# Edge batches whose rows are fetched one by one on two queues: eleven batches instead of three, and an own side in fp32

## The reference

```python
theta = x[dst] - x[src]
w = sigmoid(relu(theta @ W1 + b1) @ W2 + b2)
agg = segment_sum(w * theta, dst)
indeg = segment_sum(ones, dst)
out = layernorm(x + agg + indeg * (x @ W4 + b4))
```

## Time and profile before

| | us |
|---|---|
| median of 3 executions | 3931.05 (3930.73 to 3932.52) |
| the profiled execution, its own time | 3929.44 |
| its span, first to last instruction | 3927.6 |
| busy: PE / PE weight load / DVE / ACT / POOL | 2018.4 / 1781.0 / 2979.7 / 1255.4 / 2953.8 |
| mean granted TensorE clock, share of full speed | 0.619 |

### The profile page before, as it was taken

How to read it: one execution, slowest core, us unless ns; L and a number is a source line. 1 busy time by engine, 2 the same in 40 slices (tenths; PEclk the granted TensorE clock), 3 DMA queues, 4 the chain that set the end, 5 groups by cost and what they waited for, 6 DMA issues and landing times.

```text
span 3927.6 us, 48444 instructions
## 1 busy us (share of the span) xinstructions
PE 2018.4 (51%) x10531; PEld 1781.0 (45%) x10531; DVE 2979.7 (76%) x4855; ACT 1255.4 (32%) x2220; POOL 2953.8 (75%) x3123
## 2 busy tenths in 40 slices
PE   3245555555545555555555555555555555555554
PEld 2244444444444444444444444444444444444444
DVE  7568777777777777777777777778778777777777
ACT  1223333333333333333333333333333333333332
POOL 7777777777777777777777777777777777777776
PEclk5565665566666556665666656666666665665666
DMA  7445455555555555555555545555555555555553
GB/s 234 131 138 148 144 147 143 146 147 147 147 147 147 147 147 148 146 148 147 147 147 143 148 145 147 147 146 148 148 146 147 147 148 145 146 148 144 149 147 105
DMA packets 343028, 577.99 MB, mean 147 GB/s; under 512 B 127642, under 2 KB 216768, under 8 KB 342501
## 3 DMA queue, kind: packets, MB, share of 16 engines
q0 software_dynamic: 147264, 399.12, 36.0%
q10 hardware_dynamic: 49501, 110.40, 8.7%
q1 hardware_dynamic: 145970, 65.36, 6.2%
HBM read 549.00 MB, written 31.99 MB: 148 GB/s over the span
## 4 chain that ended last, share of the span: by engine, by line
POOL 60%; issue 24%; DVE 8%; ACTq 4%; ACT 2%; DMA 1%; PE 0%; POOLq 0%; DVEq 0%
POOL arena L783 56%; POOL held_x L768 4%; ACTq L895 3%; DVE logit L1012 2%; DVE diff L1004 2%; DVE ps_both L998 1%; DMA arena<-table,lists 1%; ACT away L875 1%; ACTq L891 1%; DVE edge_rows L1027 1%; DVE edge_rows L1017 1%; ACT hot_ne L883 0%; ACT ps_log L902 0%; DVE square L976 0%; DVE rstd L978 0%
## 5 line engine op out<-in xcount | busy, mean ns | idle before, releaser
L783 POOL DMA_INDIRECT arena<-table,lists x2970 | 2810.2, 946 | 905.0 <-issue 899.5
L875 ACT ACTIVATE away<-dst_rows,neg_ids 126x896 bf16<-126x896 bf16 (+1 forms) x449 | 466.4, 1039 | 1587.6 <-issue 1587.6
L812 PE MATMUL ps_win<-edge_rows 128*128 128x130 f32 x3140 | 716.3, 416 | 424.7 <-DVE edge_rows L1027 406.7
L812 PE MATMUL ps_sum<-edge_rows 128*128 128x130 f32 x3136 | 713.4, 415 | 422.2 <-DVE edge_rows L1027 404.3
L812 PEld LDWEIGHTS ps_win<-edge_rows 128*128 128x128 f32 x3140 | 663.2, 319 | 482.8 <-issue 482.6
L812 PEld LDWEIGHTS ps_sum<-edge_rows 128*128 128x128 f32 x3136 | 660.1, 318 | 480.2 <-issue 479.6
L998 DVE TENSOR_TENSOR ps_both<-ps_both,arena 128x896 f32<-128x896 f32 x425 | 467.0, 1099 | 485.6 <-DMA arena<-table,lists 482.0
L794 PE MATMUL ps_both<-parts,hot_ne 126*128 126x128 bf16 x3138 | 334.3, 266 | 958.7 <-ACT hot_ne L883 633.7
L794 PEld LDWEIGHTS ps_both<-parts,hot_ne 126*128 126x128 bf16 x3138 | 245.9, 118 | 1072.1 <-issue 569.7
L1027 DVE TENSOR_TENSOR edge_rows<-arena,ps_log 128x896 f32<-128x896 f32 x425 | 461.5, 1086 | 129.2 <-ACT ps_log L902 129.0
L1004 DVE SCALAR_TENSOR_TENSOR diff<-ps_both,w_rows 128x896 f32<-128x896 f32 (+1 forms) x449 | 489.4, 1090 | 15.4
(11 more groups left out here) (136 smaller groups left out, 1198.6 us busy)
## 6 DMA issues: line engine op xcount, KB each, us to landing
dst_rows<-rel_of ACTq DMA_DIRECT2D x224, 441.0 KB
arena<-table,lists POOLq DMA_INDIRECT x2970
held_x<-table ACTq DMA_DIRECT2D x2688, 1.0 KB
parts<-parts_of SPq DMA_DIRECT2D x449, 31.5 KB
parts_of<-stage SPq DMA_DIRECT2D x112, 96.0 KB, 3.4
winT<-in_x_cols SPq DMA_DIRECT2D x112, 64.0 KB
window<-in_x SPq DMA_DIRECT2D x112, 64.0 KB
out<-yout SPq DMA_DIRECT2D x112, 64.0 KB
```

The source lines that it names most:

```text
L783: nc.gpsimd.indirect_dma_start(gath[:, slot_of(g) + t, :], None, table, ids)\
L812: last = nc.tensor.matmul(ps_sums(c), hot_en[:, b, t, :], scaled_x[:, b, t, :], start=(j == 0 and t == 0), stop=(stop and t == tiles_of(g) ...
L875: nc.scalar.activation(away[0:WK, b, 0:n], dst_rows[0:WK, p % 2, lo:lo + n], ACT.Abs, bias=neg_ids[0:WK, near_no(g):near_no(g) + 1]).then_ ...
```

## The change

The own side goes from three bf16 parts to one fp32 product over all 128 rows of the window. With it go `high`, `mid`, `take_high`, `low`, the store and the loads of parts, and the near lists. `hot_ne` becomes fp32 and `own` gets two buffers.

The batches fetched by hand become eleven. The number lists of all eleven go through DRAM (`hand_of`) into one partition (`hand_at`, two buffers). Of a batch's 896 rows SyncE fetches 500 and ScalarE 396: ScalarE 11 a batch from batch 42 on, during 396 batches, issued in three groups of 3, 4 and 4 around `distance` and `one_hot`; SyncE 56 a chunk from chunk 11 on, in runs of at most 28. `project_window(c + 2)` moves from j = 2 to j = 3, and `take_window(c + 2)` from j = 3 to j = 0 of the next chunk. SyncE's order for chunk c is now: load of window c + 1, a run of 28, result c - 1, the rest.

```diff
-HAND = 3
-HAND_FROM = 40
+HAND = 11
+HAND_FROM = 42
+SPAN = 36
+ACT_EACH = 11
+SP_ROWS = BATCH - ACT_EACH * SPAN
+SP_FROM = -(-HAND_FROM // NB)
+SP_LOAD = 28
+SP_EACH = 2 * SP_LOAD
...
+        def sync_rows(c):
+            lo = (c - SP_FROM) * SP_EACH
+            runs = []
+            for m, row in [divmod(n, SP_ROWS) for n in range(lo, lo + SP_EACH) if 0 <= n < HAND * SP_ROWS]:
+                if runs and runs[-1][0] == m and runs[-1][2] < SP_LOAD:
+                    runs[-1][2] += 1
+                else:
+                    runs.append([m, row, 1])
+            return runs
...
+        def hand_numbers(kind, m, row, n):
+            return nc.values_load_multi_w_load_instructions(
+                hand_at[0:1, m % 2, row:row + n], engines=[kind], min_val=0, max_val=z.nodes - 1,
...
+        def hand_transfer(eng, m, row, number):
+            p, t = divmod(row, BT)
+            eng.dma_start(hand_x[p:p + 1, m % 2, t, :], table[bass.ds(number, 1), :])\
+                .then_inc(hand_in[2 * m + row % 2], 16)
...
+        def fetch_by_sync(sp, m, row, n):
+            if row == 0:
+                sp.wait_ge(scaled, hand_free(m))
+                sp.wait_ge(hand_at_in[m % 2], 16 * (m // 2 + 1))
+                sp.sem_inc(sp_gate, 1)
+            for k, number in enumerate(hand_numbers(mybir.EngineType.SP, m, row, n)):
+                hand_transfer(sp, m, row + k, number)
...
-            for c in range(last_chunk + 1):
-                if c < last_chunk:
-                    store_parts(sp, c + 1)
-                if c:
-                    store_result(sp, c - 1)
-            store_result(sp, last_chunk)
+            store_numbers(sp)
+            for c in range(1, last_chunk):
+                wait(sp, rows_done, c - 1)
+                sp.wait_ge(win_ready, c)
+                sp.sem_inc(sp_gate, 1)
+                bases = clamped(base_i, c - 1, c + 2, z.last_base)
+                load_window(sp, c + 1, bases[2])
...
+                rows = sync_rows(c)
+                for m, row, n in rows[:1]:
+                    fetch_by_sync(sp, m, row, n)
+                store_result(sp, c - 1, bases[0])
+                for m, row, n in rows[1:]:
+                    fetch_by_sync(sp, m, row, n)
...
-                pe.wait_ge(parts_in[buf], 16 * (g // (2 * NB) + 1))
+                pe.wait_ge(own_ready, c + 1)
...
-                    last = nc.tensor.matmul(ps_z[b][:, t, :], hot_ne[0:WK, b, t * P:(t + 1) * P],
-                                            parts[0:WK, buf, :], start=True, stop=True)
+                    last = nc.tensor.matmul(ps_z[b][:, t, :], hot_ne[:, b, t * P:(t + 1) * P], own[:, c % 2, :],
+                                            start=True, stop=True)
...
-                if j == 2 and c + 2 <= last_chunk:
+                if j == 3 and c + 2 <= last_chunk:
                     project_window(c + 2)
                 add_up(g)
...
-                if hand_row(g):
-                    fetch_hand(*hand_row(g))
+                by_hand = hand_row(g)
+                if by_hand:
+                    numbers = load_hand(*by_hand)
+                    fetch_hand(*by_hand, numbers, 0)
                 if g + 3 < all_batches:
                     distance(g + 3)
+                if by_hand:
+                    fetch_hand(*by_hand, numbers, 1)
+                if g + 3 < all_batches:
                     one_hot(g + 3)
+                if by_hand:
+                    fetch_hand(*by_hand, numbers, 2)
...
-                if j == 3 and c + 2 <= last_chunk:
-                    take_window(c + 2)
+                if j == 0 and 0 < c < last_chunk:
+                    take_window(c + 1)
```

More of the change, by code:

```diff
@@ L14 @@
 EPS = 1e-5
-ROUND = 12582912.0
 BT = 7
@@ L34 @@
 SB = 3
-SLOTS = 4
 DB = 2
@@ L100, in __init__ @@
         self.held = [c * NB for c in self.held_chunks]
-        self.hand = [HAND_FROM + (P + 2) * (m + 1) + m for m in range(HAND)]
-        assert self.hand[-1] < self.batches and HAND_FROM > self.held[1] and not set(self.hand) & set(self.held)
+        self.hand = [HAND_FROM + SPAN * (m + 1) + 2 * NB - 1 for m in range(HAND)]
+        assert self.hand[-1] < self.batches and not set(self.hand) & set(self.held)
+        assert HAND_FROM > self.held[1] and HAND_FROM + SPAN > self.held[3] and SP_EACH * SPAN >= SP_ROWS * NB and\
+            SP_FROM + -(-HAND * SP_ROWS // SP_EACH) < self.chunks
         assert min(b - a for a, b in zip([0] + self.held, self.held)) >= PAIRS * STEPS and self.groups > 16
@@ L448, in hand_row, with hand_free @@
         def hand_row(g):
[L449 to L453, removed]
+            m, n = divmod(g - HAND_FROM, SPAN)
+            return (m, SP_ROWS + n * ACT_EACH) if 0 <= m < HAND else None
+        def sync_rows(c):
[7 more added lines that the diff above has]
+            return runs
+        def hand_free(m):
+            return (z.hand[m - 2] if m >= 2 else z.held[2 * m + 1]) + 1
+        def hand_numbers(kind, m, row, n):
+            return nc.values_load_multi_w_load_instructions(
+                hand_at[0:1, m % 2, row:row + n], engines=[kind], min_val=0, max_val=z.nodes - 1,
+                skip_runtime_bounds_check_because="src holds numbers of nodes")[1]
+        def hand_transfer(eng, m, row, number):
+            p, t = divmod(row, BT)
+            eng.dma_start(hand_x[p:p + 1, m % 2, t, :], table[bass.ds(number, 1), :])\
+                .then_inc(hand_in[2 * m + row % 2], 16)
         def held_step(g):
@@ L662, in clamped, with load_window, store_result @@
                 skip_runtime_bounds_check_because="place_bases clamps it to this range")[1]
[L664 to L689, removed]
+        def load_window(sp, c, base):
             sp.dma_start(winT[:, c % 2, :], x_cols[:, bass.ds(base, P)]).then_inc(window_in[c % 3], 16)
             sp.dma_start(window[:, c % 3, :], x[bass.ds(base, P), :]).then_inc(window_in[c % 3], 16)
-        def store_result(sp, c):
+        def store_result(sp, c, base):
             sp.wait_ge(y_ready, c + 1)
@@ L882, in one_hot, with load_hand, fetch_hand @@
                 act.wait_ge(away_ready, g + 1)
-                nc.scalar.activation(hot_ne[0:WK, b, 0:n], away[0:WK, b, 0:n], ACT.Relu, bias=ones_col[0:WK, :],
+                nc.scalar.activation(hot_ne[:, b, 0:n], away[:, b, 0:n], ACT.Relu, bias=ones_col[:, :],
                                      scale=-1.0).then_inc(hot_ready, 1)
-            def fetch_hand(m, row):
-                if row == 0:
-                    act.wait_ge(scaled, (z.hand[m - 1] if m else z.held[1]) + 1)
+            def load_hand(m, row):
+                if row == SP_ROWS:
+                    act.wait_ge(scaled, hand_free(m))
+                    act.wait_ge(hand_at_in[m % 2], 16 * (m // 2 + 1))
                     act.sem_inc(act_gate, 1)
-                lo = first_tile(z.hand[m])
-                ids = nc.values_load_multi_w_load_instructions(
-                    src_at[row:row + 1, lo:lo + BT], engines=[mybir.EngineType.Activation], min_val=0,
-                    max_val=z.nodes - 1, skip_runtime_bounds_check_because="src holds numbers of nodes")[1]
-                for t in range(BT):
-                    nc.scalar.dma_start(hand_x[row:row + 1, t, :], table[bass.ds(ids[t], 1), :])\
-                        .then_inc(hand_in[2 * m + t % 2], 16)
+                return hand_numbers(mybir.EngineType.Activation, m, row, ACT_EACH)
+            def fetch_hand(m, row, numbers, part):
+                lo, hi = part * ACT_EACH // 3, (part + 1) * ACT_EACH // 3
+                for k in range(lo, hi):
+                    hand_transfer(nc.scalar, m, row + k, numbers[k])
             def gate(g):
@@ L905, in gate @@
                     .then_inc(wgt_col_ready, 1)
-            def high(c):
-                act.wait_ge(own_ready, c + 1)
-                wait(act, parts_out[c % 2], 16 * (c // 2))
-                nc.scalar.copy(stage[:, c % 2, 0, :], own[:, :]).then_inc(high_ready, 1)
-            def mid(c):
-                act.wait_ge(rest_ready, c + 1)
-                nc.scalar.copy(stage[:, c % 2, 1, :], rest[:, :]).then_inc(mid_ready, 1)
             for k in range(z.groups):
@@ L1117, in windows_vector @@
                 weigh(g)
-                if j == 1 and c < last_chunk:
-                    low(c + 1)
                 one_hot_rows(g)
```

163 lines of the change are left out of this document (53 added, 110 removed).

## The result

The changed kernel takes 4275.41 us (median; 4272.96 to 4276.60), the kernel before 3930.89. The ratio is 1.0875, with a 95% interval of 1.0856 to 1.0893: 345 us slower. The profiled execution has a span of 4273.5 us. The kernel before took 3930 to 3931 us here and in `e11`, but 4730 to 4828 us in the eleven other runs, so times are compared only where the kernel before takes about the same. First the page of the profile: the chain that ended last, by engine and by line (SPq and ACTq are the queues of SyncE and ScalarE, with register loads and DMA issues).

A forecast was written before the change was run, and what follows sets the result against it. POOL bounded the kernel before; a closed loop through SyncE, 35.55 us a chunk against 33.04, would bound the changed one. 97 intervals add 243 us, first window 4, hands' ends 10, last batches -10: 4176, forecast 4178 us, range 4010 to 4450.

The forecast's parts named there:

- Steps 1 and 2: VectorE, from take_window through scaling and difference to the end of normalise: 1.48 us plus 15.35 us a chunk.
- Step 3: SyncE, from the end of normalise to issuing the result's DMA: 0.67 us a chunk.
- Step 4: SyncE's run behind the result: loading 28 numbers (2.1 us) and 28 row DMAs (11.2 us), 13.4 us with handovers.
- Step 5: SyncE's next chunk: waits and base, second window DMA, then landing of the window's data: 3.8 us.
- Step 6: TensorE's project_window, 0.65 us, plus 0.2 us of handovers: 0.85 us a chunk.
- the hands' ends: Chunks where a hand ends: first run cut short, run behind the result 24 rows longer over all: about +10 us.
- The stretch behind batch 436: Last 12 batches: POOL has worked ahead, VectorE sets the pace at about 7.5 us a batch: -10 us.
- the reading of 0.58 us for each group of four touched: ScalarE's register load: 0.58 us per aligned group of four numbers touched, so 2.0 us for eleven numbers.
- A: Rival: SyncE's run of 28 takes under 10.2 us, POOL stays the bound, 3859 us; chance 0.07.
- B: Rival: ScalarE becomes the bound at 8.3 us a batch, SyncE's load not late, about 3935 us; chance 0.04.
- C: Rival: single rows share one place at 0.40 us each, 4605 us; chance 0.09, including runs of rows beyond the bounds.
- the loop: Closed chain through SyncE once a chunk, window to result to row run to next window and projection: 35.55 us.

The follow-up runs named there:

- e11: Changed kernel with the three hand batches and old fetch of the kernel before put back (fp32 own side, moved window, SyncE's order kept): 3930.04 us against 3930.23.
- e8: Changed kernel with SyncE fetching only the rows behind the result, 28 a chunk, those ahead left out: 6090.5 us.
- e9: Changed kernel with SyncE fetching only the rows ahead of the result, 28 a chunk, those behind left out: 5052.9 us.
- e5: Changed kernel with window c + 2 loaded right after result c - 1, ahead of the second run of rows: 5784.1 us, kernel before 4730.0.
- e6: The changed kernel itself again, nothing altered, on a chip where the kernel before takes 4791.6 us: 5972.4 us.
- e10: The kernel before itself, unaltered, profiled on a slower chip: 4827.7 us.

## Why the prediction was right

The forecast was 4178 us, the measured time 4275; the direction, the mechanism and its place were right, and the loss was undersized, 247 us of 345. Step by step, with the turn printed above and, in the sum, the averages over 97 turns:

- **Steps 1 and 2, VectorE.** 16.83 us were summed, 16.96 measured (2009.75 to 2026.71, the end of `normalise`).
- **Step 3, the result's DMA.** 0.67 us, measured 0.61.
- **Step 4, the run.** 13.4 us. It took 13.9 (2027.32 to 2041.22): 28 rows at 0.418 us instead of 0.40. Its load took 1.99 us of the 2.2 ahead of the first row; the 2.1 us assumed were near. The 5.6 us by 200 ns a register (the Trainium skill, "Runtime: NRT & Kernel Launch", section "Instruction fetch mechanics") fell. That page speaks of loads from HBM; these come from SBUF, and here the measurement decides.
- **Step 5, the window.** 3.8 us, measured 3.87 to the start of the projection. Within it the base took longer and the landing was shorter: 2.17 us from the second issue, where 2.6 had been set.
- **Step 6, the projection.** Here the sum went most wrong in proportion: 0.85 us against 1.25. TensorE stands idle for 14 us ahead of it, and the two matmul instructions then take 1.22 us, where the earlier trace rows had 0.65. Nearly all of the difference goes with the granted TensorE clock. Below are the stretches around the projection, first two of the kernel before, then the turn's idle stretch of TensorE and its projection; the columns are length, busy time and number of PE, PEld, DVE, ACT and POOL, the clock, DMA share, GB/s.

```profile
2018.70:2019.60 0.90, 0.76 (x7) 0.36 (x4) 0.81 (x1) 0.29 (x2) 0.59 (x2) 1.00 0.21 81
2185.60:2187.20 1.60, 1.60 (x8) 1.20 (x7) 1.50 (x6) 0.09 (x1) 1.17 (x2) 0.50 0.26 82
```
```profile
2031.00:2044.90 13.90, 0.00 (x0) 0.00 (x0) 5.21 (x6) 4.67 (x8) 10.41 (x12) 0.58 0.53 150
2044.90:2046.40 1.50, 1.31 (x4) 1.14 (x5) 0.06 (x1) 0.48 (x1) 1.03 (x2) 0.50 0.29 89
```

  The row that gave the price ran at the upper of the clock's two levels. The one at 2185.82 us ran at the lower and took 1.16 us, so the trace of before had both prices: of its 97 projections from 600 us on, 42 began at the lower level. In the changed kernel all 97 did, each behind an idle TensorE, and took 1.22 us; in the turn shown the clock fell while TensorE was idle, from 1.00 at 2029 to 2031 us, where it was busy.
- **The sum.** 36.59 us in this turn, 36.77 on average, against 35.55. By step, on average: VectorE 0.15 us more than forecast, the run 0.50 (13.90), the window 0.21 (4.01), the projection 0.41 (1.26), the result's DMA 0.04 less. The 1.2 us are 118 us over 97 turns, more than the whole miss of 97; 48 of them are the run's and 40 the projection's. The 10 us added apart for the hands' ends are in the run's 48, since the turns there are longer. The stretch behind batch 436 gave back 22 us (10 expected), which brought the number nearer by luck; the first window cost 6 (4 expected).
- **Waits.** The profile shows what was named: idle time ahead of L1005, POOL waiting for TensorE. VectorE's wait was 9 to 10 us a chunk where I wrote 5 to 7.
- **ScalarE.** It fits, as expected. Its load of 11 numbers took 2.57 us at the median and 1.38 only where the first number stood at a multiple of four, so 2.28 us on average, where 2.0 was assumed: three loads in four were dearer. So the reading of 0.58 us for each group of four touched fell: three groups took 1.38 us from a multiple of four and 2.57 us from one place behind it.

```profile
L443 ACTq TENSOR_LOAD <-hand_at x396: 1367/2566/2698, 559.5 to 4190.2; - x198
L443 SPq TENSOR_LOAD <-hand_at x206: 472/1670/2130, 565.7 to 4181.0; - x103
```

- **Rivals.** A (POOL stays the bound) fell on its own condition: a row cost 0.418 us, not 0.29. B fell with it. C (a shared place that takes 0.40 us a row) fell as well: SyncE kept 0.418 us a row while ScalarE issued its own, 11 rows every 7.4 us where nothing held it, and 100 rows in 36.77 us are 0.37 us a row. In the trace each of the 9856 rows is one packet of 1,024 bytes, and it took 55 to 56 ns on average.
- **What carries the mechanism.** The trace of the changed kernel shows the loop by itself, and `e11` shows that nothing else in the change costs time, both on chips where the kernel before takes 3930 us. `e8` against `e9` shows, where it takes near 4800, that the place of the rows and not their number makes the loop. That another order on SyncE would win back the 345 us on a chip like that of the result is not shown. The gain that the change was after, 70 us at POOL, stays an estimate from 2914 gathers in place of 2970: no run had it.

## What to carry to other kernels

When small jobs are given to a queue that seems idle, read its list in order and ask which transfer stands behind them, and who waits for that. If the answer leads back to the event that releases the jobs, the queue's idle time is no room for the jobs; add up one turn of the loop, with each step's row. And price a step that will come after a pause by a row that also comes after a pause, and look at the clock granted in both: here the same two matmul instructions took 0.65 us at the upper level and 1.16 to 1.22 at the lower.

## What was not expected

- The registers' loads go by place as much as by number: on ScalarE 11 numbers cost 1.37 to 1.43 us from a multiple of four and 2.54 to 2.70 us otherwise. On SyncE 28 numbers, always from a multiple of four, cost mostly 1.64 to 2.0 us.
- The same kernel took 3930 us and 4730 to 4828 us, both on one chip at different times (4730 in `e5`, 3930 in `e11`). The gathers kept 946 ns. The queues lost: in the changed kernel the mean step between two rows on SyncE went from 0.42 to 0.74 us (`e6`), with steps of about 0.7, 1.4 and 2.1 us among the regular ones. The kernel before shows the like on ScalarE (`e10`) with no single row on SyncE, so it is not rival C. What causes it stays open.
- With the own side in fp32 the mean granted TensorE clock was 0.807 of full speed in `e11`, where the kernel before had 0.619, and both took the same time.
